# One-core attention, LSTM and mixture-of-experts kernel: fetched rows of blocks 11 to 18 in another buffer, row fetches spread between row writes, and more filler products in the routing

## What is computed

```
gates = softmax(tokens @ wg);  expert = argmax(gates)
pos   = rank of the token among those of its expert
keep  = pos < capacity                      # 1.25 * 2048 / 8 = 320 rows
h     = relu(rows_of_expert @ w1[e] + b1[e])      # 320x128 @ 128x512
out   = x + gate * (h @ w2[e] + b2[e])            # for kept tokens; x for the others
```

## Time and profile before

| | us |
|---|---|
| median of 3 executions | 735.28 (735.28 to 737.05) |
| profiled execution, whole | 732.37 |
| profiled execution, span | 730.5 |
| PE busy | 671.1 (92%) |
| DVE busy | 449.8 (62%) |
| ACT busy | 337.1 (46%) |
| POOL busy | 120.8 (17%) |
| mean granted clock of PE | 0.961 |

### The profile page before, as it was taken

The page is one execution under the profiler, slowest core; times in us unless marked ns, Lnnn a source line. Parts: engine busy times, 40 slices in busy tenths (PEclk is TensorE's granted clock), DMA queues, the critical chain, the costliest instruction groups (busy, mean ns, idle before and its releaser), DMA issues.

```text
span 730.5 us, 16700 instructions
## 1 busy us (share of the span) xinstructions
PE 671.1 (92%) x6573; PEld 575.7 (79%) x6579; DVE 449.8 (62%) x1177; ACT 337.1 (46%) x914; POOL 120.8 (17%) x221
## 2 busy tenths in 40 slices
PE   6699999999999999989999998999999999777595
PEld 2487778988988889967777676999999999574574
DVE  5499857748756656689999998333343444531343
ACT  1589852333222222357888786455554544101121
POOL 2225730040000000034000010000000000037434
PEclk9899999999999999999999999999999999858699
DMA  8500200000000000033322100000000010402100
GB/s 256 180 20 17 62 2 1 1 1 1 1 1 1 1 1 0 9 96 85 92 67 68 36 7 2 1 2 1 15 9 23 1 26 13 93 20 84 30 20 22
DMA packets 30088, 25.03 MB, mean 34 GB/s; under 512 B 3887, under 2 KB 26801, under 8 KB 29762
## 3 DMA queue, kind: packets, MB, share of 16 engines
q1 hardware_dynamic: 28418, 20.91, 10.2%
q0 software_dynamic: 1600, 3.15, 1.4%
HBM read 19.33 MB, written 5.51 MB: 34 GB/s over the span
## 4 chain that ended last, share of the span: by engine, by line
PE 79%; DVE 9%; issue 3%; SPq 3%; another core or an unknown queue 2%; ACT 1%; DMA 1%; POOLq 0%; POOL 0%; DVEq 0%
PE SC L692 16%; PE PT L702 12%; PE MI L619 5%; PE SC L879 5%; PE PT L609 5%; PE SC L600 3%; PE SC L797 3%; PE SC L839 2%; PE SC L968 2%; PE SC L844 2%; PE SC L803 2%; PE PJ L582 2%; PE SC L800 2%; PE PT L850 2%
## 5 line engine op out<-in xcount | busy, mean ns | idle before, releaser
L1097 ACT ACTIVATE big<-SC 128x512 f32<-128x512 f32 x88 | 52.6, 600 | 144.5 <-PE SC L692 144.4
L702 PEld LDWEIGHTS PT<-wd,big 128*128 128x128 f32 (+1 forms) x768 | 90.2, 191 | 2.8 <-issue 0.4
L702 PE MATMUL PT<-wd,big 128*128 128x128 f32 (+1 forms) x768 | 90.7, 274 | 0.0
L1424 DVE TENSOR_TENSOR big<-SC,big 128x512 f32<-128x512 f32 (+1 forms) x88 | 60.6, 689 | 41.7 <-PE SC L692 32.4
L692 PE MATMUL SC<-xP,wgP 128*128 128x512 f32 x264 | 78.8, 407 | 0.7 <-DVE big L1424 0.3
L692 PE MATMUL SC<-xP,wuP 128*128 128x512 f32 x264 | 74.6, 391 | 0.0
L692 PEld LDWEIGHTS SC<-xP,wuP 128*128 128x128 f32 x264 | 49.5, 188 | 10.9
L619 PEld LDWEIGHTS MI<-vblk,PTs 128*64 128x64 f32 x1536 | 49.3, 138 | 10.9 <-ACT oT L1044 2.8
L619 PE MATMUL MI<-vblk,PTs 128*64 128x18 f32 x1536 | 53.8, 213 | 3.9 <-ACT big L1049 1.7
L1039 ACT ACTIVATE PTs<-PT 128x512 f32<-128x512 f32 x96 | 52.2, 595 | 7.1 <-PE PT L609 6.1
L609 PE MATMUL PT<-ident,sc 128*128 128x128 f32 x384 | 54.0, 285 | 0.6 <-ACT sc L1034 0.6
(11 more groups left out here) (257 smaller groups left out, 1293.5 us busy)
## 6 DMA issues: line engine op xcount, KB each, us to landing
kvs<-in_ctxT SPq DMA_DIRECT2D x32, 64.0 KB, 1.9
w1s<-in_e1w SPq DMA_DIRECT2D x8, 256.0 KB, 2.9
w2s<-in_e1w SPq DMA_DIRECT2D x8, 256.0 KB, 3.1
wg<-in_wg SPq DMA_DIRECT2D x1, 1408.0 KB, 9.1
wu<-in_wu SPq DMA_DIRECT2D x1, 1408.0 KB, 12.0
wd<-in_wd SPq DMA_DIRECT2D x2, 512.0 KB, 14.1
x_mid<-X SPq DMA_DIRECT2D x1, 1024.0 KB, 5.1
X<-x_mid SPq DMA_DIRECT2D x4, 256.0 KB, 4.8
```

What stands on the lines that cost most here:

```text
L702: last = pe.matmul(PT[:, e % 2, t * P:t * P + P], h[0:w, t * P:t * P + P], wd[0:w, e, c, :], start=(c == 0), stop=(c == 2))
L1097: act.activation(sg[a % 2], SC[:, a % 2, :], ACT.Silu).then_inc(s["silu_done"], 1)
L1424: last = dve.tensor_tensor(hT[e % 2][0:w, c, :], SC[0:w, 2 + a % 2, :], sg[a % 2][0:w, :], ALU.mult)
```

## The change

Five edits. (1) The rows of blocks 11 to 18 go to `big`, columns 2048 to 4095. (2) POOL fetches the blocks of experts 0 to 2 first (blocks 0 to 7), and then, for each expert e, those of expert e+3 ahead of the writes of expert e; the wait for `out_stored` stands behind the first eight fetches. (3) POOL's product with the gates waits for all four pieces of the lanes' one-hot. (4) Fillers: 12 become 25, 5 become 9, two new ones stand behind the sums, 13 new ones behind the rank counts. (5) `BURST` is 12 instead of 10.

```diff
-BURST = 10
+BURST = 12
+AHEAD = 3
...
-               + [wd[:, e, 0:2, :].rearrange("p c d -> p (c d)") for e in range(E0)] + [spent[:, 7 * P:9 * P]])
+               + [big[:, 2048 + 256 * i:2304 + 256 * i] for i in range(8)] + [spent[:, 7 * P:9 * P]])
...
+            pool.wait_ge(s["lane_ready"], NT // 4)
             pool.tensor_tensor(gate_at, in_block, v1[:, :].unsqueeze(2).broadcast_to([P, NT, NQ]), ALU.mult
...
-            for q in range(NQ):
-                pool.indirect_dma_start(xin[q], None, rows_in,
...
-            pool.wait_ge(s["out_stored"], 64)
-            for e in range(E1):
+
+            def gathers(e):
+                for q, r, _, _ in parts_of(e):
+                    if r == 0:
+                        pool.indirect_dma_start(xin[q], None, rows_in,
...
+            def scatters(e):
                 for j, (q, _, _, w) in enumerate(parts_of(e)):
                     if e % 2 == 1 or w == P:
                         pool.wait_ge(s["y_ready"], 3 * e + j + 1)
                         pool.indirect_dma_start(out, bass.IndirectOffsetOnAxis(ap=home[:, q:q + 1], axis=0),
...
+            for e in range(AHEAD):
+                gathers(e)
+            pool.wait_ge(s["out_stored"], 64)
+            for e in range(E1):
+                if e + AHEAD < E1:
+                    gathers(e + AHEAD)
+                scatters(e)
...
-            keep_warm(SC[:, 1, :], 12)
+            keep_warm(SC[:, 1, :], 25)
             rows_t(3, 11, NT)
...
-            keep_warm(SC[:, 1, :], 5)
+            keep_warm(SC[:, 1, :], 9)
...
                       ).then_inc(s["sums_done"], 1)
+            keep_warm(SC[:, 1, :], 2)
             pe.wait_ge(s["sums_copied"], 1)
...
                 expert_out(e, p)
+            keep_warm(SC[:, 1, :], 13)
             pe.wait_ge(s["token_ready"], 1)
```

More of the change, by code:

```diff
@@ L523, in _ @@
             pool.wait_ge(s["home_ready"], 1)
-            for q in range(NQ):
-                pool.indirect_dma_start(xin[q], None, rows_in,
-                                        bass.IndirectOffsetOnAxis(ap=home[:, q:q + 1], axis=0),
-                                        bounds_check=T - 1, oob_is_err=False).then_inc(xin_loaded[q * P // CAP], 16)
-            pool.wait_ge(s["out_stored"], 64)
-            for e in range(E1):
+            def gathers(e):
+                for q, r, _, _ in parts_of(e):
+                    if r == 0:
+                        pool.indirect_dma_start(xin[q], None, rows_in,
+                                                bass.IndirectOffsetOnAxis(ap=home[:, q:q + 1], axis=0),
+                                                bounds_check=T - 1, oob_is_err=False).then_inc(xin_loaded[e], 16)
+            def scatters(e):
                 for j, (q, _, _, w) in enumerate(parts_of(e)):
```

## The result

Four runs of each kernel on one chip: 724.15 us median (723.67 to 725.48) against 735.51 us before (735.28 to 737.05). The ratio is 0.985 (95% interval 0.983 to 0.987): faster by 11.4 us, where I forecast 22.4 and 713. The direction was right, and the time lies in my range, but the size is half. The profiled execution took 724.5 us with a span of 722.7.

A forecast was written before the change was run, and what follows sets the result against it. Bound: the chain behind the LSTM, with PE at half clock in the routing and a hold behind expert 0. Routing 8.9 plus hold 13.5 makes 22.4 us off 732.4, 710.0; with the median 2.9 higher, 713; range 708 to 728.

The forecast's parts named there:

- What bounds the kernel: Chain behind the LSTM: half clock on PE through ranks and sums, and PE's signals 12.6 us late behind the first expert.
- fetches three experts ahead: POOL's fetches and writes in the experts: the hold behind expert 0 and its half clock go, 13.5 us less, cost zero.
- Rival D: In the experts: the hold returns with each group of fetches, up to 12.6 us each; one leaves 725.5; chance 0.06.
- 25 fillers for 12: PE's wait for the last normed rows: 5.4 us of fillers end 0.3 us ahead of the rows and cost nothing.
- 9 for 5: PE ahead of the one-hot matrix: nine fillers at full clock take 1.9 us, PE ready about with the matrix, gain 0.7.
- Ranks: From PE's turn of the matrix to DVE's first rank step, 3.97 us: full clock saves 1.35, DVE's chain takes back 0.1.
- Home sums: PE's 32 home products at 0.11 instead of 0.22 us each, at full clock: 3.5 us less.
- Gate sums and burst: PE ahead of the experts: gate sums 3.5 us less at full clock; 12 burst fillers instead of 10 cost zero.
- rival A: Clock lost within the sums, about one us into the gate sums: first expert 4.4 to 5 us later, 717.3; chance 0.24.
- POOL's gate product behind the lanes: Routing: an estimated 0.5 us off DVE's four pieces, 0 taken for the start; the product hidden with 0.6 us to spare.
- The place in `big`: Fetched rows put in another column, same bytes and partitions: zero effect.
- Rival B: Behind the first expert: the hold comes with the first output products and stays whole, 726.4, or 731 with A; chance 0.20.

## Why the prediction was right or wrong, point by point

*What bounds the kernel: right in the trace that I read, wrong as a property of the kernel.* The hold of 12.6 us was real, and so was the half clock. But the hold is in the traces of some chips only: where before takes 735 us, not where it takes 724. Nothing in one profile could say so. Without holds the order of the fetches brings nothing (ratio 1.001) and the whole step of 13.5 us is void; a chance for "the hold is not always there" was missing among my rivals. The first comparison does not say which chip it ran on; by its 735.5 us and the holds in both its traces it was one with holds.

*The step that failed most: "fetches three experts ahead", 13.5 us.* It gave 6.82. I had argued that POOL's writes and fetches, 6.5 us an expert against PE's 5.9, cost nothing because no row would be late. No row was late. But the holds came back with that load, as the kernel without writes shows (48.8 us for the experts; with the writes 55.7 in the first comparison, 57.5 on this same chip). I had used the load to check the landing times and not the hold that I wanted to remove. Rival D came nearest, with a chance of 0.06: its sign, several remote waits that each end with a group of fetches, was there. But groups of fetches alone do not hold, and it had the price too high (12.6 us for each hold, measured some 1 to 4).

*"25 fillers for 12": right in cost, wrong in effect.* They fitted, with 0.34 us to spare where I had 0.3. But behind them come five turns, a rest and ten products of eight columns, and the clock fell to half at 635.7 all the same. They have a gain that I gave at nothing, since my trace did not show it: they keep the clock full through the last rows' turn, 1.2 us against the other traces of before. With it the routing gives 4.7 us (38.15 - 33.49) where the traces of the first comparison show 2.65.

*"9 for 5": wrong sign.* I had them at 1.9 us, full clock, and a gain of 0.7. They ran at half, 3.65 us, and PE came to the one-hot matrix 2.09 us after DVE had it (639.40 against 637.31, the end of its comparison) where it was 0.95 before: 1.1 us lost. Five at half clock would have ended some 1.7 us sooner (4 x 0.43, an estimate; it was not run by itself).

*Ranks: right in kind.* 2.97 us from the turn to DVE's first rank step where it was 3.97, because the clock was back at 639.1: 1.0 of the 1.3 expected. The working had PE's steps at 2.7 us; by the timeline they were 3.3, and fell to 2.1.

*Home sums: right.* 3.72 us for 6.99, 0.11 us a product, and home 3.3 us sooner by that.

*Gate sums and burst: wrong, and rival A right.* A had the clock fall about one us into the gate sums; it fell as they began, at 649.35. The sums took 6.99 us as before, and the 12 fillers 3.9 where 10 had taken 3.0. (A's time of 717.3 supposed that the hold was gone.) Sum of the routing: 0.4 (logits) - 1.1 + 1.0 + 3.3 + 0.0 - 0.9 = 2.7 us for my 8.9. A alone would have left 4.4; the nine fillers and the burst took the rest. The landing of the rows, which I put at 1.5 us behind the third fetch, was not what the first expert waited for; where it was, with one pass for both sums, it took 2.0 us.

*POOL's gate product behind the lanes: right.* DVE's four pieces took 3.05 us instead of 3.58, the product 0.73 instead of 1.17, and it was ready at 648.2, a us ahead of the gate sums.

*The place in `big`: right, zero.* *The time of the profiled execution against the median:* it stood 3.1 us low before and 0.4 high after, which is the 3.5 us between the 7.8 of the spans and the 11.4 of the medians.

*Rival B (the hold comes with the first output products) is refuted* by the kernel that fetches all rows first on a chip with holds: 743.27 us, and outputs as on a chip without them.

## What to carry to other kernels

Before a stall that the trace attributes to nobody carries the larger half of a forecast, look at it on a second chip, or give "not always there" a chance of its own. Whether the clock is full at a given step can also differ between traces of one program, so read that step in more than one trace. Fillers paid here for what stood right behind them: the last rows' turn, the ranks and the home sums. Within the thin products further on the clock was lost again, and fillers that then ran at half clock stood in the way at twice their length. Two passes of thin products with the same weights cost by the instruction here, so put their columns side by side.

## What the runs showed of the hardware that I had not expected

- On one identified chip (before 735.5 to 736.3 us), and on that of the first comparison, signals of PE reach ACT and DVE up to 12.6 us late; on two other chips (before 723.8 to 724.3 us) the same programs show none (on the second of them only the changed kernel and the one with one pass left traces), even beside 27 DMAs of POOL without a pause, and on a third the kernel before takes 727.1 us. On the chips with holds they came only with POOL's indirect DMAs in a long run beside a PE at work: 20 fetches, or fetches and writes by turns. How long is not one number: the first signal that comes late is due 14 us behind the first fetch in the trace of before, and 5 us behind POOL's first write in that of the changed kernel. Ten fetches ahead of the experts, groups of three fetches with pauses, or writes in groups leave the signals on time. PE's instructions go on being issued meanwhile. The ends of PE's records are modelled, so the trace cannot tell a late signal from products that end late. What holds them back is open: queue, port or the recording of the trace itself, since every time here comes with a record of clock and span. It was not tried to make PE issue fewer instructions in that stretch.
- The Trainium skill, SBUF — State Buffer, section on the two separate sides, says that a DMA cannot slow a compute operation. PE's instructions go on being issued during the holds here, which agrees as far as it goes. Of late signals the page says nothing, and no run here shows whether the products behind them ended late. My reading of it as a case for rival B went too far: B fell (743.27 us).
- A sum over 16 tiles with 20 columns took 3.72 us at full clock, one with 40 columns 4.30 to 4.96 with part of it at half. In the part at full clock 12 instructions start in each us with either width: the price is the instruction, not the column.
- The same untouched code up to the LSTM's end took 625.0 to 631.7 us in the profiles, more than most parts of this change are worth.
